# Copying transposed probabilities out of PSUM in pairs in a fused cross-attention and ternary feed-forward kernel

## What is computed

```python
# attention, per batch item b; input1 = layernorm(x), input2 = ctx
theta_x = einsum('ld,bdt->btl', theta_w, input2) + theta_b
phi_x   = einsum('ld,bdt->blt', phi_w, input1) + phi_b[:, None]
p       = softmax(einsum('btl,bls->bts', theta_x, phi_x))     # 512 x 512
g_x     = einsum('ld,bdt->btl', g_w, input1) + g_b
t_x     = einsum('bts,bsl->blt', p, g_x)
h       = relu(layernorm over (l, t) of t_x, with gamma and beta)
x       = x + tanh(g0) * (einsum('ol,blt->bot', out_w, h) + out_b + input2)
# feed-forward with ternary weights and 8-bit activations
y       = layernorm(x)
x       = x + tanh(g1) * bitlinear(silu(bitlinear(y, w1)) * bitlinear(y, w2), w3)
```

## Time and profile before

| | us |
|---|---|
| median of 3 runs | 312.59 (312.37 to 313.79) |
| the profiled execution: device time | 312.92 |
| the profiled execution: span from first to last instruction | 309.9 |
| outside the span (difference) | 3.0 |
| PE busy | 298.2 (96%) |
| DVE busy | 240.3 (78%) |
| ACT busy | 196.2 (63%) |
| POOL busy | 195.9 (63%) |
| chain that ended last: PE / ACT / DVE / issue | 70% / 15% / 9% / 4% |

### The profile page before, as it was taken

One profiled execution on the slowest core, in us unless ns is written; L12 is line 12 of the kernel. 1 busy time (PEld: TensorE's weight loads), 2 busy tenths in 40 slices (PEclk: granted clock), 3 DMA queues, 4 the chain that ended last, 5 costly groups with the idle time before them and its releaser, 6 DMA issues.

```text
span 309.9 us, 4392 instructions
## 1 busy us (share of the span) xinstructions
PE 298.2 (96%) x1345; PEld 161.4 (52%) x1362; DVE 240.3 (78%) x515; ACT 196.2 (63%) x343; POOL 195.9 (63%) x297
## 2 busy tenths in 40 slices
PE   8999999999999999999897999999999999999994
PEld 8766657575757665444343444444444444444451
DVE  3897878796969795877698798787976896768572
ACT  1498999789999837665953644736465546355430
POOL 3360959584949177683458878778686786655510
PEclk9999999999999999999999999999999999999999
DMA  7999953545020001010305433354234561642242
GB/s 261 418 414 413 384 211 139 203 135 205 0 69 0 0 6 30 1 36 1 68 2 102 103 63 91 85 122 117 53 83 102 71 119 52 138 102 48 54 102 102
DMA packets 50518, 36.45 MB, mean 118 GB/s; under 512 B 40896, under 2 KB 41024, under 8 KB 49472
## 3 DMA queue, kind: packets, MB, share of 16 engines
q1 hardware_dynamic: 50352, 36.05, 39.8%
q10 hardware_dynamic: 144, 0.13, 0.3%
HBM read 22.02 MB, written 4.19 MB: 85 GB/s over the span
## 4 chain that ended last, share of the span: by engine, by line
PE 70%; ACT 15%; DVE 9%; issue 4%; POOL 0%; DVEq 0%; ACTq 0%; POOLq 0%
PE bank L1023 30%; PE bank L1042 17%; ACT wq L435 5%; PE bank L969 4%; PE bank L951 4%; ACT prob L482 4%; PE bank L938 3%; PE bank L982 3%; PE bank L962 3%; ACT probT L478 2%; PE bank L1048 2%; PE bank L920 2%; DVE stage L733 1%; DVE x L675 1%; PE bank L930 1%
## 5 line engine op out<-in xcount | busy, mean ns | idle before, releaser
L1023 PE MATMUL bank<-wq,stage 128*128 128x512 bf16 x498 | 113.2, 379 | 3.4 <-DVE stage L733 2.7
L1023 PEld LDWEIGHTS bank<-wq,stage 128*128 128x128 bf16 x512 | 49.8, 98 | 65.9 <-DVE stage L733 5.2
L733 DVE SCALAR_TENSOR_TENSOR stage<-bank,s,stage 128x512 f32<-128x512 f32 x64 | 47.7, 745 | 30.7 <-PE bank L1023 20.6
L507 ACT ACTIVATE xn<-stage 128x1024 f32<-128x1024 f32 x32 | 33.8, 1057 | 47.8 <-DVE stage L733 47.8
L1042 PE MATMUL bank<-wq,prob 128*128 128x512 bf16 x253 | 57.4, 379 | 1.1 <-ACT prob L583 1.0
L501 ACT ACTIVATE stage<-bank,s 128x512 f32<-128x512 f32 x64 | 42.7, 680 | 21.3 <-PE bank L1023 19.2
L374 POOL TENSOR_SCALAR stage<-stage,hsc 128x1024 f32<-128x1024 f32 x30 | 33.4, 1122 | 21.5 <-DVE hsc L753 21.5
L307 POOL TENSOR_SCALAR prob<-prob,rsum 128x512 f32<-128x512 f32 x32 | 21.6, 693 | 35.8 <-DVE rsum L639 35.8
L1042 PEld LDWEIGHTS bank<-wq,prob 128*128 128x128 bf16 x256 | 25.0, 98 | 30.9 <-issue 0.9
L738 DVE TENSOR_REDUCE m<-stage 128x1 f32<-128x1024 f32 x32 | 38.9, 1216 | 0.8
L951 PE MATMUL bank<-ph,th 128*128 128x512 f32 x96 | 36.0, 488 | 0.0
(11 more groups left out here) (107 smaller groups left out, 421.7 us busy)
## 6 DMA issues: line engine op xcount, KB each, us to landing
c_sb<-ctx_in_dram SPq DMA_DIRECT2D x8, 512.0 KB, 3.9
stage<-w1t_dram SPq DMA_DIRECT2D x4, 1024.0 KB, 12.3
stage<-w2t_dram SPq DMA_DIRECT2D x4, 1024.0 KB, 14.7
stage<-w3t_dram SPq DMA_DIRECT2D x4, 1024.0 KB, 5.4
out_dram<-stage SPq DMA_DIRECT2D x16, 256.0 KB, 2.3
x<-x_dram SPq DMA_DIRECT2D x7, 512.0 KB, 11.7
pc<-pack_c_dram SPq DMA_DIRECT2D x1, 640.0 KB, 16.6
x<-x_dram SPq DMA_DIRECT2D x2, 256.0 KB, 3.6
```

Source lines behind the costliest of these rows:

```text
L507: A.activation(junk, h_sb[t % 2][:, half * HF:(half + 1) * HF], ACT.Square, accum_out=ssq[:, half:half + 1]).then_inc(sq_done, 1)
L733: V.scalar_tensor_tensor(h_sb[k][:, c * 512:(c + 1) * 512], up_banks(n)[1][:, :], s12[:, u % 2, 1, k:k + 1], sil[n % 3], ALU.mult, ALU.mul ...
L1023: last = mm(bank[:, :], turned[:, row:row + P], wq[:, at:at + 512], start=q == 0, stop=q == KI - 1)
```

## The change

The two banks for transposed probabilities become one PSUM tensor, `turned`, of 1024 columns. The 32 ACT copies of 512 columns become 16 copies of 1024 columns, each waiting for two turns. On PE the turns, the scores and the values of the loop are put in pairs. On ACT both score blocks 0 and 1 are exponentiated between the two copies. The semaphore `pT_ready` counts pairs.

```diff
-        banks = [ps(f"bank{n}", [P, 512]) for n in range(8)]
+        banks = [ps(f"bank{n}", [P, 512]) for n in range(4)]
+        turned = ps("turned", [P, 1024])
+        banks += [turned[:, 0:512], turned[:, 512:1024]] + [ps(f"bank{n}", [P, 512]) for n in (6, 7)]
...
-            def p_copy(i, c):
-                act.wait_ge(pT_done, 4 * i + c + 1)
-                A.copy(probT[:, c % 2], b_pt[c % 2][:, :]).then_inc(pT_ready, 1)
+            def p_copy(i, half):
+
+                act.wait_ge(pT_done, 4 * i + 2 * half + 2)
+                A.copy(probT[:, :, :].rearrange("p k t -> p (k t)"), turned[:, :]).then_inc(pT_ready, 1)
...
                 if i >= 1:
                     p_copy(i - 1, 0)
+                exp(i, 0)
+                exp(i, 1)
+                if i >= 1:
                     p_copy(i - 1, 1)
-                exp(i, 0)
-                if i >= 1:
-                    p_copy(i - 1, 2)
-                exp(i, 1)
                 slot(i, 5)
-                if i >= 1:
-                    p_copy(i - 1, 3)
                 exp(i, 2)
...
-                if 4 * i + c >= 2:
-                    pe.wait_ge(pT_ready, 4 * i + c - 1)
+                if c % 2 == 0 and 4 * i + c >= 2:
+                    pe.wait_ge(pT_ready, 2 * i + c // 2)
...
             def values(i, c):
-                pe.wait_ge(pT_ready, 4 * i + c + 1)
+                pe.wait_ge(pT_ready, 2 * i + c // 2 + 1)
...
             values(B - 1, 0)
+            values(B - 1, 1)
             turn_p(B - 1, 2)
-            values(B - 1, 1)
             turn_p(B - 1, 3)
             values(B - 1, 2)
             values(B - 1, 3)
```

More of the change, by code:

```diff
@@ L542, in _ @@
             p_copy(B - 1, 1)
-            p_copy(B - 1, 2)
-            p_copy(B - 1, 3)
             relu(B - 2)
@@ L1007, in up @@
                 elif n == 2:
-                    pe.wait_ge(pT_ready, 4 * B)
+                    pe.wait_ge(pT_ready, 2 * B)
                 elif n == 5:
@@ L1062, in _ @@
                     turn_p(i - 1, 0)
+                    turn_p(i - 1, 1)
                 scores(i, 0)
@@ L1065, in _ @@
                     var_mm(i - 2)
-                if i >= 1:
-                    turn_p(i - 1, 1)
-                    values(i - 1, 0)
                 scores(i, 1)
                 if i >= 1:
+                    values(i - 1, 0)
+                    values(i - 1, 1)
                     turn_p(i - 1, 2)
-                    values(i - 1, 1)
+                    turn_p(i - 1, 3)
                 scores(i, 2)
-                if i >= 1:
-                    turn_p(i - 1, 3)
-                    values(i - 1, 2)
                 scores(i, 3)
                 if i >= 1:
+                    values(i - 1, 2)
                     values(i - 1, 3)
```

## The result

| | before | changed |
|---|---|---|
| median device time | 312.68 us (4 runs, 312.37 to 313.79) | 318.09 us (4 runs, 317.71 to 318.79) |
| ratio | | 1.0169, 95% interval 1.0136 to 1.0202 |
| profiled execution | 312.92 us, span 309.9 | 317.74 us, span 315.3 |

I had forecast 316.0, in a range of 313.9 to 317.8. The sign and the place were right; the amount was 2 us short and just outside the range.

A forecast was written before the change was run, and what follows sets the result against it. In repeats 4 to 6 PE is nearly full, but the end of ACT's last exponential sets the repeat. Terms 0.2 + 3 x 0.58 + 0.16 + 1.35 = +3.4 us, from the median of 312.59, gave 316.0; range 313.9 to 317.8.

The forecast's parts named there:

- the price of the wide copy: ACT's 1024-column copy: 0.90 us from start to start, bounds 0.84 and 1.03, against two copies of 0.47.
- After the loop: Item 7's turns to `up(0, 1)`: no scores cover the copies, so the pair stands in the open twice; +1.35 us.
- Repeats 1 and 2: Loop start: shrinking or earlier waits against values 0 behind a longer copy; +0.2 us, between -0.4 and +0.6.
- The closed loop: Repeats 4 to 6: third turn, ACT's unbroken queue, last exponential, `add_out`, `out_proj(., 1)`; PE already waits 0.27 us there.
- Repeats 4 to 6: Full loop repeats: last exponential 0.58 us later, at 9.42 instead of 8.84 behind the first turn; +1.7 us for three.
- Repeat 3: Loop repeat with slots 5 and 6 empty: exponentials wait for `row_max`, scores 3 come 0.85 earlier; 0 us.
- Repeat 7: Last loop repeat: exponential 2 starts when `row_max(2)` ends, at 6.56 instead of 6.40 behind the first turn; +0.16 us.
- a delay passes whole: Behind 132.5 us the chain through PE and DVE has no slack, so a delay arrives at the end unchanged.
- the cause is not the copy: Full repeats: the 0.58 us comes from ACT idling until turn 3 with slot 5 queued behind that wait.
- The first rival: Loop: the 0.58 us does not reach PE, leaving the tail and 0.16; +1.5, 314.1 us; chance 0.15.
- The faster rival: ACT is the bound and PE's waits go, if the pair copy starts before 4.6; 310.6 us; chance 0.05.
- The slower rival: PE also waits at values 2 or theta, +0.3 us in seven repeats; 318 us; chance 0.10.

The follow-up runs named there:

- e2: Changed kernel with ACT's 1024-wide piece of weight work (slot 5) moved from behind the second copy to between exponentials 0 and 1; 314.77 us, ratio 1.0063.
- e5: Kernel before, with ACT's piece of weight work (slot 5) moved from behind exponential 1 to directly behind exponential 0; 311.62 us, ratio 0.9960.
- e6: As e5, with the relu of item i-2 also moved ahead of the fourth copy, against the kernel before; 310.77 us, ratio 0.9940.
- e4: Changed kernel with its new order kept, each wide copy split into two 512-column copies with their own signals; 314.47 us, ratio 1.0048.

## Why the prediction was wrong by 2 us

The mechanism of the loop was right, and terms of the sum were mis-sized. The step that failed is the price of the wide copy for PE: I charged its distance to ACT's next instruction, 0.90, where PE waits for its whole duration and the signal, 1.06. After the loop that is 0.32 of the 0.51 us by which the term was too small (1.86 measured for 1.35), and a slower start of the values behind a wait is the rest. Repeats 1 and 2, in which PE waits for the first copy too, stood in the sum at 0.2 and took 0.58.

Right, by its steps:
- *The closed loop.* Third or fourth turn, ACT's queue, last exponential, `add_out`, `out_proj(., 1)`: e2, e5 and e6 move only work on ACT, end the last exponential earlier and shorten the repeats; the change ends it later and lengthens them.
- *Repeats 4 to 6.* Second copy at 5.24 forecast, 5.27 measured; last exponential at 9.42, measured 9.45; repeats 16.2, measured 16.19 and 16.20; PE wait 0.8, measured 0.83. Forecast +1.7, measured +1.78.
- *Repeat 3.* Forecast 0, measured +0.05. The copies of the loop are hidden from PE in repeats 3 to 7, as said, and theta of the next item is not held up.
- *The copy.* 0.90 from start to start, measured 0.90 to 0.92 (0.95 once, in repeat 1). From the figures of the Trainium skill's page "ScalarE: Activation LUTs", section "What ACT_TABLE_LOAD costs", its duration comes to 0.186 + 1024 x 0.00083 = 1.04 us, an estimate; the rows have 1.01 to 1.04, on average 1.017.

Too small:
- *After the loop: +1.35 forecast, +1.86 measured.* The mechanism was right, the term was mis-sized. PE's values start at 131.91, 1.06 behind the copy's start at 130.85, and not 0.90. That is 0.16 twice. And values that start after a wait take 1.83 for the pair and not 1.72 (131.91 to 133.74), 0.11 twice. Together 0.54, where 0.51 was missing. With the 0.11 goes a difference in the weight loads (PEld): after the wait the first one starts with its values at 131.91, while in repeat 3, without a wait, it starts 0.23 ahead of values at 54.73. That this is the cause was not tested.

```profile
54.50 0.43 PEld L967 LDWEIGHTS bank<-probT,gs 128*128 128x128 f32 x2
...
131.91 0.30 PEld L967 LDWEIGHTS bank<-probT,gs 128*128 128x128 f32 x2 [1.07 <-ACT probT L481]
```

- *Repeats 1 and 2: +0.2 forecast, +0.58 measured.* The first copy holds PE up in both: 0.21 in repeat 1, and about 0.30 in repeat 2, where values start 1.08 behind the scores ahead of them (37.34 to 38.42) and 0.78 behind them in repeat 3. The view of waits doesn't list that one; the rows are

```profile
37.33 1.04 ACT L481 COPY probT<-turned 128x1024 f32<-128x1024 f32 x1
...
38.42 1.98 PE L967 MATMUL bank<-probT,gs 128*128 128x512 f32 x4
```

What failed beside the copy's price is that I weighed repeat 2 by eye: its last exponential came 0.7 later against G (9.14 before, 9.86 now), where a full repeat has 0.6, and +0.6 was my upper end for both repeats together. The wait of 0.48 at `mean_mm` between them also did not come earlier: it is 0.62 now.
- *Repeat 7: +0.16 forecast, +0.30 measured.* Again a start-to-start distance for a duration: exponential 2 waits for `row_max(2)` to end, 0.69 plus the signal, not 0.61. It started 6.71 behind G, not 6.56.
- *Not in the sum at all:* +0.25 after `up(0, 1)`, where I had said that a delay passes whole: it grew on the way, in a wait for DVE that goes with the wide copies of item 7. And +0.59 at the start, which is a DMA's landing time in this execution. Whether it belongs to the medians is open: they differ by 5.4 and the lengths without the start by 4.8, while for the seven other kernels the two agree to about 0.3, and all four executions of the changed kernel have a span of 315.3 us or more.
- *Wrong in kind:* "the cause is not the copy". Its cost on ACT is not the cause; its width is, in part. Run e4 splits the length's 4.8 us into 1.8 for the order and 3.1 for the width, because one instruction begins after both turns and signals after both banks. I had folded this into the order, since the pair of turns was in both. In a full repeat the order takes 0.4 of the 0.6 and the width 0.2; after the loop the width takes 1.4 of 1.9, and the 0.25 behind it; the other 0.8 of the width are in repeats 1 and 2.

The first rival (absorbed) fell by the trace, since the PE wait is there. The faster rival fell by ACT's busy time, 196.0 against 196.2, and by its own sign, a second copy before 4.6: it starts at 5.27. The slower rival's number, 318, is what was measured, but by luck: it asks for PE waits at values or theta in seven repeats, and none is seen in repeats 3 to 7. The Trainium skill's page "Perfetto Trace Analysis", section "Optimizing Scalar/DVE Operations", says that breaking instructions up may let work finish sooner where ScalarE or VectorE is not saturated but makes others wait. Run e4 agrees: twice the copies, and 3.1 us less by length.

## To carry to other kernels

Grouping two transfers between engines saves one instruction's fixed cost (here 0.03 us a pair) and costs the overlap of the first half's transfer with the making of the second half. Price both, and the second where the consumer waits. Where an in-order engine pauses for another, what stands behind the pause in its queue counts as much as what it waits for: look for work that could stand ahead of it. Use the distance from start to start for an engine's own queue, but the whole duration plus the signal wherever another engine waits.

## What I had not expected of the hardware

- A copy of 1024 columns that reads two PSUM banks took 1.017 us on average against 0.590 for 512, and 0.91 against 0.47 from start to start: 0.43 to 0.44 us for 512 columns more, and only about 0.03 of fixed cost saved.
- Two values right after a wait for the copy took 1.82 to 1.83 us to the next start, without a wait 1.72.
- `tx_norm` on DVE, 0.74 us in repeat 4 before, took 1.00 in the changed kernel, at a place where POOL was busy, while before it was idle there. No chain went through it, and what made it slower was not tested.
